# A Mamba layer and its experts in one program: the states of the scan multiplied and summed in columns on VectorE instead of through transposes

## What is computed

```python
xin = in_proj_w @ context;  u = silu(causal_conv4(xin) + conv_b)      # 512 channels x 512 positions
dt_lo, B, C = split(x_proj_w @ u);  delta = softplus(dt_proj_w @ dt_lo + dt_b)
for l in positions:                                                    # 16 states n for each channel
    state = state * exp(delta[l] * A) + (delta[l] * u[l]) * B[l]
    y[l] = sum_n(state * C[l])
y = (y + D * u) * silu(layernorm(x))                                   # z = layernorm(x)
x = x + tanh(g_xattn) * y
h = layernorm(x)
out = expert(h, shared) + sum_e w_e[row] * expert(h, e)                # 7 routed, top 3 have weight
x = x + tanh(g_ffn) * out                # expert = (silu(h @ W1) * (h @ Wg)) @ W2, all 512 x 512
```

## Time and profile before

| | us |
|---|---|
| median of 3 runs | 1517.13 (1515.59 to 1517.44) |
| the profiled execution, its own time | 1515.26 |
| its span, first to last instruction | 1513.2 |
| mean granted TensorE clock in it | 0.961 of full |
| HBM read and written | 207.39 MB and 57.93 MB |

### The profile page before, as it was taken

How to read it: one execution, slowest core, us unless ns; L and a number is a source line. 1 busy time by engine, 2 the same in 40 slices (tenths; PEclk the granted TensorE clock), 3 DMA queues, 4 the chain that set the end, 5 groups by cost and what they waited for, 6 DMA issues and landing times.

```text
span 1513.2 us, 18790 instructions
## 1 busy us (share of the span) xinstructions
PE 1396.1 (92%) x6311; PEld 1078.1 (71%) x6311; DVE 1053.7 (70%) x1259; ACT 509.7 (34%) x855; POOL 454.0 (30%) x240
## 2 busy tenths in 40 slices
PE   8598879999999959999999958999999999999999
PEld 4244456877777846787777846787877878888887
DVE  5888875898899764689999855589999852322222
ACT  3666535544444212532233112533223111111111
POOL 4200023678777611122332211123233211111111
PEclk9599989999999978999999988999999999999999
DMA  6122723765776563455555553455555554655542
GB/s 204 42 63 63 273 117 141 285 225 215 263 243 235 191 220 114 151 184 180 182 178 178 188 209 90 151 194 176 173 181 175 169 199 141 220 195 194 193 167 83
DMA packets 90808, 266.46 MB, mean 176 GB/s; under 512 B 11472, under 2 KB 11600, under 8 KB 90336
## 3 DMA queue, kind: packets, MB, share of 16 engines
q1 hardware_dynamic: 85472, 258.39, 50.2%
q10 hardware_dynamic: 5248, 6.96, 1.3%
HBM read 207.39 MB, written 57.93 MB: 175 GB/s over the span
## 4 chain that ended last, share of the span: by engine, by line
PE 71%; DVE 15%; ACT 5%; issue 5%; DMA 2%; SPq 1%; ACTq 0%; DVEq 0%
PE ps_hg L457 19%; PE ps_h L457 18%; PE ps_y L457 12%; PE ps_y L608 8%; DVE st L1094 7%; PE ps_mid L534 5%; DVE y_rows L1100 3%; PE ps_h L526 2%; ACT dA L787 2%; DMA st<-xin_scratch 1%; DVE st L1085 1%; PE ps_mid L504 1%; PE ps_mid L497 1%; PE ps_mid L500 1%; DVE h_tmp L1215 1%
## 5 line engine op out<-in xcount | busy, mean ns | idle before, releaser
L1357 POOL TENSOR_TENSOR h_lo<-h_tmp,h_hi 128x512 fp32r<-128x512 f32 x128 | 280.8, 2194 | 799.7 <-ACT h_hi L859 799.7
L457 PE MATMUL ps_h<-x_hi,w_split 128*128 128x512 f32 x1024 | 352.8, 406 | 7.2 <-DVE x_lo L1147 4.3
L457 PE MATMUL ps_hg<-x_hi,wg_split 128*128 128x512 f32 x1024 | 348.3, 401 | 0.0
L1094 DVE TENSOR_TENSOR_SCAN st<-dA,st 128x1024 f32<-128x1024 f32 x128 | 298.4, 2341 | 0.0
L457 PE MATMUL ps_y<-w_split,h_hi 128*128 128x512 f32 x1024 | 256.4, 398 | 0.8 <-ACT h_hi L859 0.8
L457 PEld LDWEIGHTS ps_h<-x_hi,w_split 128*128 128x128 f32 x1024 | 196.5, 192 | 49.7 <-issue 5.2
L859 ACT ACTIVATE h_hi<-h_tmp 128x512 fp32r<-128x512 f32 x128 | 81.0, 633 | 425.7 <-DVE h_tmp L1220 425.7
L457 PEld LDWEIGHTS ps_hg<-x_hi,wg_split 128*128 128x128 f32 x1024 | 194.8, 190 | 40.7 <-issue 0.3
L457 PEld LDWEIGHTS ps_y<-w_split,h_hi 128*128 128x128 f32 x1024 | 189.0, 189 | 39.6 <-ACT h_hi L859 2.0
L1215 DVE SCALAR_TENSOR_TENSOR h_tmp<-h_tmp,ps_h 128x512 f32<-128x512 f32 x128 | 87.8, 686 | 183.9 <-ACT h_tmp L853 183.3
L457 PE MATMUL ps_h<-x_lo,w_split 128*128 128x512 f32 x512 | 203.1, 397 | 0.0
(11 more groups left out here) (140 smaller groups left out, 1130.7 us busy)
## 6 DMA issues: line engine op xcount, KB each, us to landing
w_split<-split_scratch SPq DMA_DIRECT2D x192, 512.0 KB, 4.8
wg_split<-split_scratch SPq DMA_DIRECT2D x96, 512.0 KB, 4.3
split_scratch<-w_split SPq DMA_DIRECT2D x64, 512.0 KB, 4.2
...
```

What stands on the lines that cost most here:

```text
L457: mm = pe.matmul(out_, lhs[a], rhs[c], start=first and q == 0, stop=last and q == len(sides) - 1)
L1094: dve.tensor_tensor_scan(flat[1], flat[0], flat[1], 0.0, ALU.mult, ALU.add).then_inc(scan_done, 1)
L1357: pool.tensor_tensor(h_lo[:, j, :], h_tmp[j % 2][:], h_hi[:, j, :].bitcast(F32), ALU.subtract).then_inc(hl_ready, 1)
```

## The change

- In batches 0 to 2 the states are no longer transposed. VectorE multiplies the state in place by C, broadcast over the channels (`cmul`, 128x2048), and adds it to `yacc` (the same memory as `y_rows`, now in columns) with `add_state` (128x2048). C comes by the DMA that brings B: `load_bc` loads both rows, 512 KB instead of 256 KB, into `bc_pair`, and waits for the `cmul` two states back.
- `slot` has one call for both products, one for `add_state` of the state before and the first scan, one for the second scan, one for `cmul`.
- D*u is made by ScalarE from u into `yacc` (`front_init`), the matmuls `init`, `ccols` and `z` of the batches go, and z stays in columns. y is multiplied by z in columns, transposed once for each sample (`y_to_rows`, 16 transposes in step 7), and the residual reads it from PSUM.
- The next convolution's input is loaded into `dA[0]` after the scans of state 14. Its first tap stands in step 7 on ScalarE, two more taps stand between the `acc` additions of step 7 on VectorE. For sample 1 ScalarE's tap and all of VectorE's stand behind `x_hi` and `x_lo`.
- SP's queue has `load_xin`, `load_x_rows` and `load_x` ahead of the weights of the next batch; in the prologue `load_x_rows(0)` stands behind the weights of step 1. The loop over batches 1 and 2 is written out.
- The prologue's way of summing (through TensorE and ScalarE) stays.

```diff
         def conv_in(m, et):
-            return st[1][:, et, :] if some(m) else conv_ps[et][:]
+            return dA[0][:, et, :] if some(m) else conv_ps[et][:]
...
             def load_xin(m):
-                sp.wait_ge(y_ready, T * m)
-                sp.dma_start(st[1][:], xin_dram[bass.ds(m, 1)].rearrange("a p t l -> p (a t) l")).then_inc(xin_ld, 16)
+                sp.wait_ge(scan_done, 2 * (DS * m - 1))
+                sp.dma_start(dA[0][:], xin_dram[bass.ds(m, 1)].rearrange("a p t l -> p (a t) l")).then_inc(xin_ld, 16)
...
+            def load_bc(m, n):
+                if n < RING:
+                    sp.wait_ge(xd_st, 16 * (m + 1))
+                else:
+                    sp.wait_ge(cmul_done, DS * (m - 1) + n - RING + 1)
+                src = xd_dram[m].rearrange("(c n) l -> n c l", c=2)[bass.ds(n, 1)].broadcast_to([P, 2, L])
+                sp.dma_start(bc_pair[n % RING][:], src).then_inc(bc_ld[n % RING], 16)
...
             store_down(0)
-            load_x_rows(0)
             load_up(1, 0)
             load_down(1, 0)
+            load_x_rows(0)
...
+            def y_to_rows(m):
+                pe.wait_ge(y_ready, T * (m + 1))
+                for i in range(T):
+                    bank, before = mid(m, row_place(i))
+                    mid_free(bank, before)
+                    for et in range(T):
+                        mm = pe.transpose(ps_mid[bank][:, et * P:(et + 1) * P], yacc[:, et, i * P:(i + 1) * P], ident[:])
+                    mm.then_inc(mid_done[bank], 1)
...
             def batch(b, m):
                 shared_step(b, m)
-                step_(STEPS * b + 1, lambda g: front(m, *{4: ("z2",), 5: ("z3",)}.get(g, ())))
-                for e in range(2, NE):
-                    step_(STEPS * b + e, state_sums(m, 3 * (e - 2)))
-                step_(STEPS * b + NE, state_sums(m, DS - 1))
+                for e in range(1, NE):
+                    step_(STEPS * b + e)
+                step_(STEPS * b + NE, lambda g: y_to_rows(m) if g == 6 else None)
...
-            def sum_rows(m, n, i):
-                bank, before = mid(m, sum_place(m, n, i))
-                dve.wait_ge(mid_done[bank], before + 1)
-                dve.scalar_tensor_tensor(out=y_rows[:, i, :], in0=ps_mid[bank][:], scalar=c_cols[:, i, n:n + 1],
-                                         in1=y_rows[:, i, :], op0=ALU.mult, op1=ALU.add).then_inc(mid_read[bank], 1)
+            def cmul(m, n):
+                odd = n % 2
+                dve.wait_ge(scan_done, 2 * (DS * m + n + 1))
+                dve.tensor_tensor(st[odd][:], st[odd][:], bc_pair[odd][:, 1:2, :].broadcast_to([P, T, L]),
+                                  ALU.mult).then_inc(cmul_done, 1)
+            def add_state(m, n):
...
+                dve.tensor_tensor(yacc[:], yacc[:], st[n % 2][:], ALU.add).then_inc(ysum_done, 1)
             def slot(m, n, r):
+                if r == 1 and n >= 1:
+                    add_state(m, n - 1)
                 if r == 0:
-                    if n >= 2:
-                        sum_rows(m, n - 2, T - 1)
-                elif 1 <= n <= DS:
-                    sum_rows(m, n - 1, r - 1)
-                if n < DS:
-                    (bmul if r % 2 == 0 else scan)(m, n, r // 2)
+                    for h in range(2):
+                        bmul(m, n, h)
+                elif r < 3:
+                    scan(m, n, r - 1)
+                else:
+                    cmul(m, n)
```

More of the change, by code:

```diff
@@ L223, in conv_in @@
         def conv_in(m, et):
-            return st[1][:, et, :] if some(m) else conv_ps[et][:]
+            return dA[0][:, et, :] if some(m) else conv_ps[et][:]
         def bcast(a, n):
             return a.rearrange("(a n) -> a n", a=1).broadcast_to([P, n])
-        FRONT = ["xproj", "init0", "dt0", "init1", "dt1", "ccols", "dt2", "init2", "dt3", "init3", "z0", "z1", "z2", "z3"]
-        FIRST_FRONT = [name for name in FRONT if not name.startswith("init")]
-        MID_FIRST = len(FIRST_FRONT) + T * DS + T
-        MID_TURN = len(FRONT) + T * DS + T + 2
-        assert MID_FIRST % 2 == 0 and MID_TURN % 2 == 0
+        FIRST_FRONT = ["xproj", "dt0", "dt1", "ccols", "dt2", "dt3", "z0", "z1", "z2", "z3"]
+        FRONT = ["routerc", "routerr", "xproj", "dt0", "dt1", "dt2", "dt3"]
+        MID_FIRST = [(len(FIRST_FRONT) + T * DS + T) // 2] * 2
+        MID_TURN = [(len(FRONT) + 2 * T + 1) // 2, (len(FRONT) + 2 * T) // 2]
         def mid(m, place):
-            o = place + (2 if some(m) else 0)
-            before = o // 2 + (MID_FIRST // 2 + MID_TURN // 2 * (m - 1) if some(m) else 0)
-            return o % 2, before
+            bank = place % 2
+            return bank, place // 2 + (MID_FIRST[bank] + MID_TURN[bank] * (m - 1) if some(m) else 0)
         def taken(m, place):
@@ L411, in _ @@
                 if n + 2 < DS:
-                    load_b(1, n + 2)
+                    load_bc(1, n + 2)
+            load_xin(2)
+            load_x_rows(1)
+            load_x(2)
             store_down(NE)
-            load_x_rows(1)
             fetch_up(1, 0)
             fetch_down(1, 0)
-            with sp.Fori(1, NB - 1) as b:
+            for b in range(1, NB - 1):
                 m = b + 1
-                load_xin(m)
-                load_x(m)
                 fetch_up(b, 1, (0, 1, 2))
                 store_xd(m)
-                load_b(m, 0)
-                load_b(m, 1)
+                load_bc(m, 0)
+                load_bc(m, 1)
                 fetch_up(b, 1, (3,))
@@ L497, in front @@
                             mm = pe.matmul(ps[0:XP, :], xproj_w[:, et, :], u[:, et, :], start=et == 0, stop=et == T - 1)
-                    elif kind == "init":
-                        for et in range(T):
-                            mm = pe.matmul(ps[:, et * P:(et + 1) * P], u[:, et, i * P:(i + 1) * P], diag_D[:, et, :],
-                                           start=True, stop=True)
                     elif kind == "dt":
@@ L796, in first_scale @@
             def first_scale(n, i):
-                bank, before = mid(0, sum_place(0, n, i))
+                bank, before = mid(0, sum_place(n, i))
                 if n:
@@ L964, in _ @@
             decays(0, 0, T)
[L965 removed]
+            first_z(range(T))
             decays(0, T, 2 * T)
@@ L974, in _ @@
                     stage(2 + (n - 1) // T, (n - 1) % T)
-            batch(0, 1)
-            with act.Fori(1, NB - 1) as b:
+            for b in range(NB - 1):
                 batch(b, b + 1)
@@ L1264, in _ @@
                 if n >= 2:
-                    bank, before = mid(0, sum_place(0, n - 2, T - 1))
+                    bank, before = mid(0, sum_place(n - 2, T - 1))
                     dve.wait_ge(mid_done[bank], before + 1)
@@ L1330, in batch @@
                 step_(STEPS * b + NE, NE - 1, last)
-            batch(0, 1)
-            with dve.Fori(1, NB - 1) as b:
+            for b in range(NB - 1):
                 batch(b, b + 1)
@@ L1385, in batch @@
                 step_(STEPS * b, split, lambda j: power(zvar, zrstd, m) if j == 1 else None)
[L1386 to L1391 removed]
+                for e in range(1, NE):
+                    step_(STEPS * b + e, split)
                 step_(STEPS * b + NE)
@@ L1418, in _ @@
             power(x2var, x2rstd, 0)
-            batch(0, 1)
-            with pool.Fori(1, NB - 1) as b:
+            for b in range(NB - 1):
                 batch(b, b + 1)
```

193 lines of the change are left out of this document (117 added, 76 removed).

## The result

The changed kernel takes 1585.98 us (median of 4 runs, 1582.54 to 1586.65), the kernel before 1516.79 beside it (1515.59 to 1517.44). The ratio is 1.0453, 95% interval 1.0434 to 1.0471. The profiled execution took 1586.45 us with a span of 1584.7, against 1515.26 and 1513.2: 71.5 us more of span.

What follows compares the result with a forecast made beforehand. TensorE bounds the kernel before; VectorE was to become the bound in steps 2 to 6. Debits of +114.2 and credits of -51.7 give +62.5 us on 1515.3, the median 1.9 above: 1579 us, range 1537 to 1612.

Steps and rivals of the forecast that it cites:

- Steps 2 to 6: Routed steps of batches 0 to 2: +50.4 us in batch 0, +31.9 each in batches 1 and 2, together +114.2.
- The count: VectorE's own work in steps 2 to 6: three states 33.3 us plus experts' products and additions 7.5, 40.8 a step.
- The stops: GpSimd subtractions delaying VectorE's SBUF passes in steps 2 to 6, 1.07 us each: 3.2 a step in batch 1, 11.2 in batch 0.
- The idle time: VectorE waiting for the second and third tanh in steps 2 to 6: 2.2 us a step, 1.3 less in step 6.
- The clock: TensorE's granted clock falling after waits in steps 2 to 6: 0.4 us a step, between 0 and 3.
- the second rival: TensorE at 1.2 GHz for much of a step, VectorE waiting for ps_y: 50 and 57 us a step, 1628; chance 0.10.
- Ends of batches: TensorE's restart after batches 0 and 1: 6.4 us instead of 21.1 and 24.4, so -14.7 and -18.0.
- Shared steps: init, ccols and half the z transposes leave TensorE: -6 us each in batches 1 and 2, -2 in batch 0.
- Step 7: y_to_rows adds transposes and waiting, TensorE enters further ahead of VectorE: -3 us in each of three batches.
- Step 1: Ends with one state's cmul more: +1, +1 and, with GpSimd, +2 us.
- The third rival: Fewer GpSimd stops in steps 2 to 6: steps of 44.5 and 50 us, 1538 in all; chance 0.14.
- The first: Rival: nothing of GpSimd stops VectorE, batch ends decide; steps of 42.6 and 46.6 us, 1502, faster; chance 0.08.

Runs made afterwards that it cites:

- both terms out: Changed kernel with GpSimd's subtractions in the batches cut to 32 elements a partition and ScalarE's decays behind the next tanh in steps 2 to 6: 1474.4 us.
- the run with small subtractions: Changed kernel with GpSimd's subtractions in the batches (h_lo and the weights' low halves) cut to 32 elements a partition: 1497.3 us.
- the tanh first: Changed kernel with ScalarE's three decays behind the next tanh instead of ahead of it, in steps 2 to 6: 1556.5 us.
- the kernel with the ends alone: Kernel before with only the next convolution's input in dA[0], its load in step 6 and taps in step 7, sums left in rows: 1490.5 us, ratio 0.982.

## Why the prediction came out right, and where its terms were off

1579 us was predicted, in a range of 1537 to 1612; 1586 came. Over the profiled executions, 62.5 us more were predicted and 71.5 came.

- *Steps 2 to 6*: +105.2 against +114.2. The count held: 40.8 us, shown twice (45.5 less stops and idle time; 40.6 busy with both terms out). The stops were 2.6 instead of 3.2 in batch 1, because one of the three VectorE paid for cost 0.45 only: GpSimd was passed over and then ran under a product that reads PSUM. In batch 0 they were 10.8 instead of 11.2, shown by the run with small subtractions. The forecast's 11.2 had a slip in it: it counts ten stops, multiplies by 10.4, and 10.4 x 1.07 is 11.1; ten would be 10.7. The idle time was 2.1 instead of 2.2, and 1.8 of it went with the tanh first. The clock, taken at 0.4, cost nothing: it fell to 0.50 within the step, and the step did not change even with a fifth of TensorE's work gone. That was the second rival, and it is refuted: VectorE never waits for `ps_y` in steps 2 to 6.
- *The lock on the way into SBUF*: the trace bears out that a subtraction of GpSimd waits for the end of VectorE's pass and that VectorE then waits for the subtraction, 1.1 us each. The stop is a little shorter than the 1.29 us that a subtraction takes alone. The Trainium skill, SBUF — State Buffer, "Who interferes with whom", calls the contention an exclusive lock; the trace agrees, with waits that end where the pass ends. In each of steps 3 to 6 of batch 1 the first subtraction was passed over for a second pass (4.75 us, as at 793.50; 3.71 with small subtractions), while the third, also 0.8 us into a sum with a scan behind it, was not; why is open.
- *Ends of batches*: TensorE's restart gained 15.0 and 14.9 us, against -14.7 and -18.0. At the second the forecast took the end of the last batch as its model. It overlooked that 24.4 had been 3.3 more than 21.1 for a reason of its own, which the earlier trace rows shows as `issue` in the row of 915.18: the jump back of TensorE's loop, which the changed kernel still has. Writing it out took 2.9 us off that end in the kernel with the ends alone; in the changed kernel it was not tried.
- *Shared steps*: -3.9 and -3.1 against -6, and +2.6 against -2 in batch 0. TensorE is busy for all of the 52.85 us and of the 56.73 before, at a clock of 0.95 in both, so no wait ate it. The term was mis-sized: the forecast took the busy time of the groups that go (4.6 for `init` in the earlier trace rows, 1.4 for the others) as the time that they add. Groups overlap with their neighbours, and the groups of that window before add up to some 75 us of busy time in 56.7. Scaled by that, the 6.7 us of busy time that went in this window are an estimated 5.1; what makes the rest of the way to 3.9 is open. Batch 0 was not taken apart.
- *Step 7*: +1.3 us in three against -9, the worst term. Two steps 7 carry taps, and the forecast gave these 1 us. In the kernel with the ends alone, where a step 7 gained only the taps and their load, they cost 3.3 us. In the changed kernel the step 7 without taps is 30.8, a gain of 2.0 and not of 3. Why batch 0's, at 35.1, is 1.5 longer than batch 1's is open.
- *Step 1*: +0.6 us in three against +4.

Credits of 51.7 us were expected and 33.7 came; the debits were 9.0 less than expected. The two errors partly cancelled, and that the total came within 7 us of the forecast is in part luck. The third rival, fewer stops, fell with batch 0's 54 us a step, though in batches 1 and 2 the 45.5 lies halfway between its 44.5 and the forecast's 46.6. The first fell with every stop that was seen. Of the signs that the forecast named, two were missed: 46 to 47 us a step in batches 1 and 2 (45.5), and a restart within 6 to 7 us at the second end (9.5). And TensorE's longest wait in the step (4.75 us) was ended by ScalarE's `h_hi` and not by a product of VectorE.

One thing was wrong in the sum though it did not show in the result: the idle time of 2.2 us was a term beside the count. It is what the count leaves of a chain through VectorE and ScalarE that holds a step at 44.4 us when the product by C is gone. By the forecast's way of adding, such a step takes 45.5 - 6.6 = 38.9.
